# First stage of a two-layer kernel: a batch's finish put ahead of the other's norm, scans moved, weight loads moved

## The reference

```
ig, fg = ([q, k, v] @ igate_w.T + igate_b).T, ([q, k, v] @ fgate_w.T + fgate_b).T
cs = cumsum(log_sigmoid(fg))
log_D = where(causal, cs[s] - cs[t], -inf) + ig[t]
D = exp(log_D - max_t(log_D))
C = (q @ k.T / sqrt(32)) * D
h = (C / (max(|sum_t C|, exp(-max_t log_D)) + 1e-6)) @ v
x = x + (h - mean(h)) / sqrt(var(h) + 1e-5) * ln_scale
```

## Time and profile before

| | us |
|---|---|
| median of 3 runs | 566.83 |
| lowest and highest | 565.88, 569.68 |
| the profiled execution's own time | 570.13 |
| its span, first to last instruction | 568.5 |
| busy: TensorE | 543.5 (96%) |
| busy: VectorE, ScalarE, GpSimd | 324.0, 236.7, 72.6 |

### The profile page before, as it was taken

How to read it: one execution, slowest core, us unless ns; L and a number is a source line. 1 busy time by engine, 2 the same in 40 slices (tenths; PEclk the granted TensorE clock), 3 DMA queues, 4 the chain that set the end, 5 groups by cost and what they waited for, 6 DMA issues and landing times.

```text
span 568.5 us, 8405 instructions
## 1 busy us (share of the span) xinstructions
PE 543.5 (96%) x2773; PEld 454.2 (80%) x2773; DVE 324.0 (57%) x792; ACT 236.7 (42%) x440; POOL 72.6 (13%) x107
## 2 busy tenths in 40 slices
PE   7898897999999999899999999999999999999996
PEld 5677775889888888778888878888788889788886
DVE  6676789678787778763443463434553444543333
ACT  6444656447978743461122351122341122531111
POOL 6232324011502323000000000000000000000000
PEclk9998999899999999999999999999999999999999
DMA  5666337154986786200000100000100000000001
GB/s 174 194 184 180 112 96 193 37 161 167 360 294 213 220 308 205 74 1 0 1 0 1 37 2 1 0 1 0 38 0 1 1 1 29 9 1 0 1 0 39
DMA packets 29860, 47.44 MB, mean 83 GB/s; under 512 B 3392, under 2 KB 21184, under 8 KB 29440
## 3 DMA queue, kind: packets, MB, share of 16 engines
q1 hardware_dynamic: 24848, 30.14, 17.0%
q0 software_dynamic: 4848, 16.78, 9.2%
q10 hardware_dynamic: 128, 0.05, 0.0%
HBM read 40.27 MB, written 2.10 MB: 75 GB/s over the span
## 4 chain that ended last, share of the span: by engine, by line
PE 58%; issue 7%; POOL 2%; DVE 1%; POOLq 0%; DVEq 0%
PE ps L938 57%; POOL rstd L453 1%; POOL h L560 1%; PE ps L594 0%; PE ps L902 0%; DVE qr L1562 0%; DVE x L1550 0%; DVE xn L1314 0%; DVE alT L1589 0%; DVE xT L1321 0%; POOL w L549 0%; POOLq L560 0%; POOL w L551 0%; PE ps L893 0%; DVE ot L1642 0%
## 5 line engine op out<-in xcount | busy, mean ns | idle before, releaser
L938 PE MATMUL ps<-hBt,h 128*128 128x512 f32 x512 | 117.6, 390 | 0.0
L938 PE MATMUL ps<-hA,h 128*128 128x512 f32 x512 | 117.4, 390 | 0.0
L1277 ACT ACTIVATE h<-ps,scol 128x512 f32<-128x512 f32 x64 | 44.1, 690 | 175.5 <-PE ps L938 175.3
L938 PEld LDWEIGHTS ps<-hA,h 128*128 128x128 f32 x512 | 95.9, 188 | 20.5 <-DVE hA L1616 0.5
L938 PEld LDWEIGHTS ps<-hBt,h 128*128 128x128 f32 x512 | 95.8, 188 | 20.4 <-DVE hBt L1616 0.6
L938 PE MATMUL ps<-xT,w 128*128 128x512 f32 x256 | 61.8, 396 | 1.0 <-DVE xT L1321 1.0
L938 PEld LDWEIGHTS ps<-xT,w 128*128 128x128 f32 x256 | 46.3, 188 | 15.0 <-issue 5.3
L1634 DVE CAST hBt<-h 128x512 fp32r<-128x512 f32 x32 | 13.7, 427 | 73.8 <-ACT h L1277 73.8
L1634 DVE CAST hA<-h 128x512 fp32r<-128x512 f32 x32 | 13.7, 427 | 70.1 <-ACT h L1277 70.1
L453 POOL TENSOR_TENSOR rstd<-ve,mhalf 128x4 f32<-128x4 f32 x16 | 17.1, 1066 | 262.6 <-DVE ve L1309 262.6
L1260 ACT ACTIVATE silD<-ps,scol 128x512 f32<-128x512 f32 x32 | 22.0, 689 | 45.3 <-PE ps L938 45.3
(11 more groups left out here) (176 smaller groups left out, 884.3 us busy)
## 6 DMA issues: line engine op xcount, KB each, us to landing
looked<-w_all_in SPq DMA_DIRECT2D x16, 704.0 KB, 5.6
h<-w_all_in POOLq DMA_DIRECT2D x16, 512.0 KB, 6.6
V<-ctx_in SPq DMA_DIRECT2D x8, 512.0 KB, 4.5
Qb<-xT SPq DMA_DIRECT2D x64, 64.0 KB, 2.7
w<-w_all_in POOLq DMA_DIRECT2D x3, 1024.0 KB, 6.9
x<-x_in SPq DMA_DIRECT2D x4, 512.0 KB, 4.5
kstA<-ctxT_in SPq DMA_DIRECT2D x4, 512.0 KB, 4.9
kstC<-ctxT_in SPq DMA_DIRECT2D x4, 512.0 KB, 6.9
```

Source lines behind the costliest of these rows:

```text
L938: last = mm(o, a, b, start=(k == 0 and p == 0), stop=(k == n_k - 1 and p == 1))
L1277: fn(h32[:, m % 2, :], ps[:, 2 + m % 4, :], ACT.Gelu, scale=scol[:, L + 1, m:m + 1])\
```

## The change

In the first stage only.

- VectorE: `finish` no longer weaves the norm of the batch before into its steps. The norm (`head_norm`) follows when all of the finish is issued, and in the second, third and fourth batch it moves behind what else stands there (`gate_a`, `x_norm` and `floor_copy`, `x_lo`). `gate_a` now follows the finish. `gate_b` and `gate_c` move from the second batch to the third, between its two `weigh`.
- ScalarE: `log_part` moves from k = 3 to k = 4. The sums over raw weights of the second group move from k = 2 to k = 7; those of the others stay. `head_stats` has one more wait, for its own step before.
- GpSimd: `pieces` moves ahead of `h_root(Q * g, 0)` and `inv_root(g + 2)`, behind a wait for the gate rows gi and gf of the next group.
- SyncE: `lead_in` issues the first part of the gate rows when VectorE's chain has made that part (`dve_a2`), and the second part at `z_ready`.

```diff
             def lead_in(g, u):
 
-                sp.wait_ge(s["z_ready"], g + 1)
                 sp.wait_ge(s["rows_set1"], 2)
-                move_rows(sp, u)
+                for part in range(ZP):
+                    if part == 0:
+                        sp.wait_ge(s["dve_a2"], A2 * (g + 1))
+                    else:
+                        sp.wait_ge(s["z_ready"], g + 1)
+                    sp.dma_start(row_of(u, part), zp[:, part, 0, :].bitcast(F32)).then_inc(s["z_moved"], 16)
+                    sp.dma_start(columns_of(u, part), zp[:, part, 1, :].bitcast(F32)).then_inc(s["z_moved"], 16)
                 queries_in(g, u, 0)
                 queries_in(g, u, 1)
...
-                    h_root(Q * g, 0)
-                    inv_root(g + 2)
                     if u == 0:
+                        pool.wait_ge(s["gate_moved"], 32 * (g + 2))
+                        pool.sem_inc(s["pieces_go"], 1)
                         pieces(i, 1)
                     else:
                         with pool.If(i < 1):
+                            pool.wait_ge(s["gate_moved"], 32 * (g + 2))
+                            pool.sem_inc(s["pieces_go"], 1)
                             pieces(1, 0)
+                    h_root(Q * g, 0)
+                    inv_root(g + 2)
...
             def head_stats(b, par):
+                act.wait_ge(s["hstat_ready"], b)
                 act.wait_ge(s["pv_used"], b + 2)
...
+                        if k == 4:
                             more(lambda: log_part(gn))
-                        if k == 4:
                             head_stats(Q * g, 0)
...
+                        if k == 2 and u == 1:
+                            if_later(act, i, raw_sums)
+                        if k == UN - 1:
+                            if u == 0:
+                                raw_sums()
+                            else:
+                                more(raw_sums)
...
             def finish(b, par, q, norm=False):
 
 
-                if norm:
-                    centre(b - 1, (q - 1) % 2)
...
-                if norm:
-                    add_on(b - 1, (q - 1) % 2)
                 ch.settle()
...
                 ch.end()
+                if norm:
+                    head_norm(b - 1, q - 1)
...
                         weigh(g, 2 * q)
+                        if q == 2:
+                            more(lambda: gate_b(gn, state["ch"]))
+                            more(lambda: gate_c(gn, state["ch"]))
                         weigh(g, 2 * q + 1)
...
                         if q == 1:
+                            finish(b - 1, u, q - 1)
                             more(lambda: state.update(ch=gate_a(gn)))
-                            finish(b - 1, u, q - 1, norm=(u == 1))
-                            more(lambda: gate_b(gn, state["ch"]))
-                            more(lambda: gate_c(gn, state["ch"]))
-                            if u == 0:
+                            if u == 1:
+                                head_norm(b - 2, Q - 1)
+                            else:
                                 before(lambda: head_norm(last, Q - 1))
                         if q == 2:
-                            finish(b - 1, u, q - 1, norm=True)
+                            finish(b - 1, u, q - 1)
+                            x_norm(g + 2, (8, 12)[u] - 8 * i)
                             more(lambda: floor_copy(gn, 1 - u))
-                            x_norm(g + 2, (8, 12)[u] - 8 * i)
+                            head_norm(b - 2, q - 2)
                         if q == Q - 1:
-                            finish(b - 1, u, q - 1, norm=True)
+                            finish(b - 1, u, q - 1)
                             if u == 0:
                                 x_lo(g + 2, u)
                             else:
                                 more(lambda: x_lo(3, u))
+                            head_norm(b - 2, q - 2)
```

More of the change, by code:

```diff
@@ L240, in two_layers @@
             av_done xC_done d_pre d_sil d_h32 d_hi d_lo d_act d_out xD_done
-            qb0_set ndiag rrs_ready idr_ready sel_zero sel_ld tri_ld tri_set lr_set rows_set0 rows_set1 dh_own ot_ready dve_prep dve_a2 dve_unit dve_b centred dve_d pool_own act_own out_done pe_own w_ld h1_ld h2_ld""".split()
+            qb0_set ndiag rrs_ready idr_ready sel_zero sel_ld tri_ld tri_set lr_set rows_set0 rows_set1 pieces_go dh_own ot_ready dve_prep dve_a2 dve_unit dve_b centred dve_d pool_own act_own out_done pe_own w_ld h1_ld h2_ld""".split()
         s = {n: sem(n) for n in names}
@@ L268, in columns_of @@
             return Lr[ZP + part * Q:ZP + part * Q + Q, u, :, :, :].bitcast(F32)
[L270 to L273, removed]
         block = es.enter_context(nc.Block())
@@ L1173, in _, with raw_sums @@
                             head_stats(Q * g + 1, 1)
-                        if k == (UN - 1, 2)[u]:
+                        def raw_sums():
                             act.wait_ge(s["raw_here"], g + 1)
```

## The result

| | us |
|---|---|
| before, median of 14 runs | 567.74 (565.88 to 569.68) |
| after, median of 14 runs | 563.90 (560.95 to 566.01) |
| ratio, 95% interval | 0.9928 (0.9909 to 0.9948) |
| the profiled execution of after | 565.76 around a span of 564.0 |

By the ratio the kernel is faster by 4.1 us (3.8 between the medians), where 8.6 were forecast.

What follows compares the result with a forecast made beforehand. TensorE's waits and half clock in the first stage were taken as the reachable loss, 14.2 us; less 2.8, 1.8 and 1.0 this gave 8.6, so 558.2 us against the median (561.5 against the profiled execution); range 554.5 to 564.5.

Steps and rivals of the forecast that it cites:

- Rival A: First stage: clock still falls after two seams, turn_e stall and seam rest being close; gain 5.2, 561.6 us; chance 0.18.
- B: First stage, fourth batch: turn_e waits the whole 2.5 us in each group; gain 3.9, 562.9 us; chance 0.12.
- signs of being wrong: Wrong if stage two's start is right but the end isn't, or half clock or fourth-batch Qb wait stands in stage one.
- the clock: First stage, after two seams: with shorter waits no fall to half clock was expected; 3.4 us back.
- the sum: First stage: reachable losses less three costs, 14.2 - 2.8 - 1.8 - 1.0 = 8.6 us gained.
- Part 1: VectorE: finish ahead of the other batch's norm, ready 0.9 us earlier; all 5.3 us of TensorE's waits for it gone.
- Part 2: Third batch: gate_b and gate_c between the products; turn_e then stalls 1.15 us in two groups, about 0.4 in the first; cost 2.8.
- Part 3: GpSimd: weight loads behind the gate rows, 5 to 7 us earlier, off the seam's transfers; costs of 1.8 and 1.0 us remain.
- the rest at the seams: Seams between groups: TensorE still waits 0.6 us for Qb at each of three, 1.8 us in all.
- the fourth batch's Qb: First stage, fourth batch: Qb transfers now beside the moved loads and V land late; 1.0 us for all three groups.
- Rival C: Seams: Qb lands 5.3 us after issue even without loads, clock falls at two; gain about 0, 566.8 us; chance 0.10.
- D: Fourth batch: loads served before Qb, 2 to 4.6 us late per group, three clock falls; slower, 573 us; chance 0.05.

Runs made afterwards that it cites:

- loads at the group's head: Changed kernel with each set of weight loads at the head of its group's part on GpSimd, behind a landing of Qb; 574.67 us, ratio 1.0088.
- finish ahead of norm: Kernel before with only the finish put ahead of the other batch's norm, plus head_stats' wait; 567.95 us, ratio 0.9989.
- four edits at once: Changed kernel with weight loads heading each group, turn_e behind the scores, last norm ahead of first finish, k_hi right after x_hi; 571.16 us, ratio 1.0031.
- Qb ahead of V: Changed kernel with SyncE issuing the fourth batch's Qb before the next group's V; 560.91 us, ratio 0.9871.
- combined: Changed kernel with Qb issued before V, loads spread, turn_e behind the scores, last norm ahead of first finish, k_hi right after x_hi; 562.09 us, ratio 0.9895.
- loads spread: Changed kernel with the third and fourth load of each set moved behind h_root(Q * g, 0) and inv_root(g + 2); 563.74 us, ratio 0.9922.
- after again: The changed kernel unaltered, run once more on the chip of the last three experiments; 562.28 us, ratio 0.9903 to the kernel before.
- loads ahead of the loop: Changed kernel with all sixteen weight loads issued before the loop: 573.19 us, loop 86.0; also with turn_e behind the fourth batch's scores: 571.13 us, loop 85.0.

## Why the prediction was right and wrong

Right in direction: under 561.2 was wanted for "faster by over 1%", and 563.9 is 0.7% under before. The time lies in the range, which took in rivals A and B. The forecast of 558.2 was 5.7 us too low, and both of its own signs of being wrong are there: half clock in the first stage, and a wait for Qb in the fourth batch. Of the 4.5 us between 8.6 and 4.1, some 3 are the clock's and 1.5 the waits'.

- **The step that failed** is the clock: "I expect no fall of the clock: 3.4 us back". It is wrong twice. After still falls to 1.2 GHz, in the first stage twice in its first profile and not at all in its second, with the same waits in the second group. And before doesn't always fall: two of its runs at a granted clock of 1.000 took 563.1 and 564.5. The falls' share is thus a matter of how often, not of yes or no. Mean granted clock of the runs: before 0.9945 (30) and 0.9933 (19), after 0.9953 (14) and 0.9972 (8). By straight lines through each kernel's runs, at 0.999 before takes 565.1 and 564.8, after 561.4 and 561.0. That puts the gain at equal clock at 3.7 and 3.8 us. The ratios give 4.1 and 5.5, the medians 3.8 and 6.1, so the clock's part is 0.1 to 2.3 us, where 3.4 were put in.
- **From the profiled execution to the median** is part of the same step. The profiled one took 570.13, 3.3 over the median of the three runs, and had both falls; I took its losses off the median in full. It is also 1.3 us above the line through the runs of before at its own clock of 0.993 (568.8). Against 570.13 the forecast was 561.5; the fall-free execution of after took 561.76.
- **The loop at full clock** was forecast to be shorter by 8.6 - 3.4 = 5.2 us, and went from 89.95 to 84.95 and 84.7: 5.0 and 5.2. That agreement flatters the sum. The waits fall by 3.5 us only (4.1 in after's second profile) and the runs at equal clock by 3.7; the rest stands in no wait, and is about the 1.3 us by which the profiled execution of before was long. So the waits too were overestimated, by about 1.5 us, and the terms below say where. Rival A, the same with the clock still falling, is what happened (561.6 for 563.9; it had 0.18), for another reason than it gave: its two waits do stand within a few microseconds, but in the fourth batch.
- Part 1: the 5.3 us of waits for the finish did go. But they weren't part 1's to give. Alone it turns most of them into waits for Qb and Lr at the seams, and the loads' move alone turns 3.3 of them into waits for the fourth batch's Qb. I had costed the parts as if each stood alone.
- Part 2 (its own terms, 2 x 1.15 + 0.4, make 2.7 and not 2.8): turn_e waits 0.63, 1.47 and 1.42 us, 3.5 in all, for 2.8. The working was near: Er is ready 5.5 us after the end of the first weighted sum (59.41 to 64.94), 5.35 forecast, and TensorE is there after 4.05, 4.2 forecast. But the wait is not a price of its own. With turn_e moved away Qb takes its place, to the tenth, and without loads the products and the seam do.
- Part 3: the rest at the seams, 1.8 us, is 0.34 at one seam; the fourth batch's Qb, 1.0, is 1.5 (0.66 and 0.85), with landings of 4.8 and 4.5 us in the median where I took 5.3 as the longest (5.8 and 5.6 it was). Together 1.9 for 2.8: the right size with the ends changed. Two readings under it were off. The loads went out 2.8, 6.1 and 4.4 us earlier, where I had 5 to 7. And the 2.0 to 3.3 us of the earlier trace rows are not Qb with the engines to itself: V, issued just ahead of it, was still under way; by itself it lands in 2.0.
- Not in the sum: kT, 1.2 us in two waits. In before k_lo ends at 49.35 + 2.37 = 51.72, 5.1 us after the group's first exponents, in after at 53.61, 5.7 after them, and TensorE, no longer held at the seam, now comes to the keys' product first. It is the next thing late behind Qb, and I hadn't asked for it. Another 0.7 us lies in CtB at the last batch and in the issue of stage two's first product.
- The waits by themselves: 5.3 + 1.74 + 3.8 = 10.8 before, 3.5 + 1.9 + 1.2 + 0.7 = 7.3 after. The sum had 10.8 going to 5.6.
- Rival C fell: at the seam Qb lands in 2.4 us with the loads elsewhere. (Its price was off too: 6.9 us of waits and two falls off 8.6 are 1.7 us slower than before, not the same.) B fell too: turn_e waits 3.5 us and not 7.5. D's mechanism is there, at a tenth of its price (1.5 us of waits for 18.9): with the loads 1.2 us behind its first transfer Qb lands in 4.8 us (median) and not behind them all. Its landing of 7 us and more needs the loads ahead of Qb, as loads at the group's head had them in the first group, and even there TensorE waited 2.00 us.

So the failed step is the 3.4 us for the clock, with 0.1 to 2.3 in its place, and behind it the waits, which gave 3.7 for 5.2. Why the clock falls in one execution and not in the next, behind the same waits, stays open: the kernels with the longest single waits (2.9 us in finish ahead of norm, 3.3 in loads at the head, 3.9 in four edits at once) have the lowest mean clocks of those run more than once, 0.991, 0.987 and 0.991, and the two at 0.998 (Qb ahead of V, combined) have none over 1.5 in the loop. But loads spread has the waits of after again and 0.995 for its 0.997, so the runs settle no more than that rough order.

## What to carry to other kernels

A stretch at half clock in one profile is a chance, not a fixed cost: price it by how often the runs have it, and set the sum against the execution it was read from. When one wait stands in front of another, remove each alone before adding gains: here two of the changes, alone or put back, were worth 0 and under 1 us in the median, and the third 4, and the place of one set of loads gave nearly all of it. Compare short stretches at equal clock: a microsecond that seemed won by turn_e's move was the clock's. When a bulk load is moved, look at which small transfers are issued in the microsecond around its new place, and what stands ahead of them in their own queue; letting them go first took two swapped issues, and the loop was 1.1 us shorter (in the medians 1.4, not clear of noise).

## What the runs showed of the hardware

- What a Qb transfer (64 KB) takes to land goes by what was issued ahead of it. With nothing ahead, 2.0 us (Qb ahead of V). Behind V's 0.5 MB in its own queue and no loads, 2.1 to 3.4 (loads ahead of the loop). The same with 1 to 1.5 MB of loads on another queue from 1.2 to 1.3 us behind its first, 3.2 to 5.8, medians of 4.5 to 4.8 (after). With the loads out 2.1 and 1.7 us ahead of it and no V, medians of 5.3 and 6.0. Behind V and a microsecond behind the first load, 6.6 to 7.5 (loads at the group's head). The Trainium skill, "DMA: Bandwidth & Descriptors", section "Queues, rings and completion order", has the engines go round the queues packet by packet. The kernel before agrees with it: at the third seam Qb, issued at 91.19 behind all four loads, lands 6.3 us later, at 97.5, the last load at 99.1. In loads at the group's head it bought nothing: Qb landed half a microsecond after the last load.
- With four loads issued over 2.3 us or the last two of them spread over GpSimd's roots the landing is much the same, medians of 4.5 to 4.8 and 4.0 to 4.8 us. The first two left at the same place in both.
- The stretches at 1.2 GHz in the first stage lasted 3.4 us in fifteen cases, 6.8 in two (finish ahead of norm alone, loads at the group's head) and 13.7 in two (loads ahead of the loop), these around a wait of 12.8 and 12.6 us; work that took 3.4 us there takes 1.7 at full clock. Straight lines through the runs of before give some 6 us for 0.01 of mean granted clock.
